# Two-layer decoder, the bridge into cross attention: cross keys are scaled and squared from their PSUM banks, with two more banks and a new written order

## What is computed

```python
x = x + self_attention(layernorm(x))                 # 32 heads of 16, causal, ALiBi
# cross attention: 32 query heads and 8 key/value heads of 128 features, no mask in effect
q = rmsnorm(layernorm(x) @ q_proj_w.T, q_norm_w)     # per head
k = rmsnorm(ctx @ k_proj_w.T, k_norm_w)              # per head, this is what is changed
v = ctx @ v_proj_w.T
x = x + softmax(q @ k.T / sqrt(128)) @ v @ o_proj_w.T
# rmsnorm(t, w) = w * t / sqrt(mean(t * t) + 1e-5)
```

## Time and profile before

| | |
|---|---|
| median of three runs | 1003.66 us (998.44 to 1005.22) |
| the profiled execution | 1004.14 us, its span 1002.4 us |
| mean granted TensorE clock | 0.970 |
| busy share of the span | PE 90%, DVE 83%, POOL 67%, ACT 63%, PE weight loads 47% |

### The profile page before, as it was taken

How to read it: one execution, slowest core, us unless ns; L and a number is a source line. 1 busy time by engine, 2 the same in 40 slices (tenths; PEclk the granted TensorE clock), 3 DMA queues, 4 the chain that set the end, 5 groups by cost and what they waited for, 6 DMA issues and landing times. The chain is left out here.

```text
span 1002.4 us, 21446 instructions
## 1 busy us (share of the span) xinstructions
PE 900.7 (90%) x6397; PEld 466.2 (47%) x6504; DVE 832.7 (83%) x2090; ACT 635.4 (63%) x1786; POOL 673.8 (67%) x689
## 2 busy tenths in 40 slices
PE   3979997799799999999999999999677887999977
PEld 1445544344344555455555545554234454655543
DVE  6998887689985889899999999898489887777685
ACT  4788887643453666676666767666243487887551
POOL 5897878677783666667666666666086687565583
PEclk9899999799999999999999999999979999999999
DMA  8799999867543666655555555666344499776665
GB/s 350 177 180 160 165 166 184 198 102 164 92 87 93 126 119 125 119 114 126 126 126 116 118 119 126 120 127 117 83 113 106 68 169 157 144 140 117 123 131 147
DMA packets 384304, 136.32 MB, mean 136 GB/s; under 512 B 369760, under 2 KB 370400, under 8 KB 381792
## 3 DMA queue, kind: packets, MB, share of 16 engines
q1 hardware_dynamic: 384224, 135.39, 65.7%
HBM read 42.01 MB, written 2.10 MB: 44 GB/s over the span
## 5 line engine op out<-in xcount | busy, mean ns | idle before, releaser
L157 PE MATMUL bank<-w_hi,hT 128*128 128x512 f16 (+2 forms) x1024 | 319.6, 370 | 16.7 <-DVE big L903 5.7
L157 PE MATMUL bank<-w_hi,small 128*128 128x512 f16 x512 | 164.0, 382 | 9.0 <-DVE small L1561 7.9
L157 PE MATMUL bank<-w_lo,hT 128*128 128x512 bf16 (+2 forms) x458 | 167.5, 368 | 0.0
L157 PEld LDWEIGHTS bank<-w_hi,hT 128*128 128x128 f16 (+1 forms) x1024 | 100.5, 99 | 117.2 <-issue 21.3
L1387 POOL TENSOR_TENSOR small<-small,mhalf 128x4 f32<-128x4 f32 x64 | 64.8, 1013 | 134.1 <-DVE small L980 134.1
L667 POOL TENSOR_TENSOR big<-big 128x512 f16<-128x512 f32 x96 | 112.8, 1182 | 33.8 <-DVE big L946 20.2
L1488 ACT ACTIVATE small<-small 128x128 f32<-128x128 f32 x256 | 98.8, 390 | 0.0
L157 PE MATMUL bank<-w_lo,small 128*128 128x512 bf16 x235 | 89.8, 382 | 0.0
L1403 POOL TENSOR_TENSOR w_lo<-stage,w_hi 128x512 bf16<-128x512 f32 x64 | 84.8, 1325 | 1.1 <-ACT w_hi L1524 1.1
L829 ACT ACTIVATE big<-bank,small 128x128 f32<-128x128 f32 x256 | 72.0, 377 | 20.7 <-DVE small L935 20.6
L1540 DVE TENSOR_TENSOR small<-small 128x512 f16<-128x512 f32 x64 | 79.4, 1240 | 4.6 <-ACT small L1483 4.4
(11 more groups left out here) (208 smaller groups left out, 2146.9 us busy)
## 6 DMA issues: line engine op xcount, KB each, us to landing
stage<-in_weights SPq DMA_DIRECT2D x16, 1024.0 KB, 5.7
stage<-in_weights SPq DMA_DIRECT2D x64, 256.0 KB, 2.9
big<-big SPq DMA_TRANSPOSE x168, 3.4
small<-in_ctxT SPq DMA_DIRECT2D x2, 1024.0 KB, 9.0
big<-in_ctx SPq DMA_DIRECT2D x2, 1024.0 KB, 5.7
out<-x SPq DMA_DIRECT2D x8, 256.0 KB, 2.4
big<-in_vectors SPq DMA_DIRECT2D x5, 256.0 KB, 9.7
x<-in_x SPq DMA_DIRECT2D x2, 512.0 KB, 5.5
```

The lines of the kernel that those rows point to most:

```text
L157: last = nc.tensor.matmul(out, lhs(a, c), rhs(b, c), start=start and n == 0, stop=stop and n == 3 * chunks - 1)
```

## The change

1. `key_scale` reads the key bank itself and not `kf[m]`. `key_stats` takes one factor from the bank and the other from `kf[m]`, so `key_take` stays. `rms_stats` gets a second source; the cross queries pass the same tile twice, as before.
2. `key_take` waits for the squares of batch b - 1 (`squares`) and no longer for `scaled`.
3. The product of `key(m, b)` waits for `scaled` of the last user of its bank and no longer for `k_taken`. Batches 0 to 3 use banks 4 and 5. From batch 4 on even batches use banks 6 and 7, odd ones 4 and 5, so the last user is then two batches back; `key_0_4` waits for the last `o_taken`. The first scores of the cross loop wait for all `scaled`.
4. Two guards are added, on `key_root` (the last `key_scale` of this m has read the root) and on `key_stats` (the last root has read the sums).
5. In the opening the product `k` of a batch waits for that batch's rows too, as `q` did.
6. All five lists of `BRIDGE_ORDER` are replaced. They hold the same steps.

```diff
-                if n == 0 and what == "q" and isinstance(b, int):
+                if n == 0 and what in ("q", "k") and isinstance(b, int):
                     opening.wait_rows(pe, b)
...
-def rms_stats(nc, dve, src, junk, ss, eps_out, chain, k):
+def rms_stats(nc, dve, src, again, junk, ss, eps_out, chain, k):
...
-        last = nc.vector.tensor_tensor_reduce(out=junk[:, at], in0=src[:, at], in1=src[:, at], scale=1.0, scalar=0.0,
+        last = nc.vector.tensor_tensor_reduce(out=junk[:, at], in0=src[:, at], in1=again[:, at], scale=1.0, scalar=0.0,
...
+FEW = 3
...
+    def key_bank(self, m, b):
+
+        return self.kbank[m if b <= FEW or b % 2 else 2 + m]
...
             if what == "key_root":
                 pool.wait_ge(self.var, b * 2 + (m + 1))
+                after(pool, self.scaled, b * 2 + (m - 1))
...
-                after(pe, self.k_taken, b * 2 + (m - 1))
-                product(self.nc, self.kbank[m][:], context(self.chip, b), columns(self.chip.weight(self.k_slots[m])),
+                if b == FEW + 1:
+                    pe.wait_ge(layer.signals["o_taken"], NB * 2)
+                else:
+                    last_user = b - 1 if b <= FEW else b - 2
+                    after(pe, self.scaled, last_user * 2 + (m + 1))
+                product(self.nc, self.key_bank(m, b)[:], context(self.chip, b), columns(self.chip.weight(self.k_slots[m])),
...
             if what == "key_take":
                 act.wait_ge(self.k_done, b * 2 + (m + 1))
-                after(act, self.scaled, b * 2 + (m - 1))
-                nc.scalar.activation(self.kf[m], self.kbank[m][:], ACT.Copy).then_inc(self.k_taken, 1)
+                after(act, self.squares, b * 2 + (m - 1))
+                nc.scalar.activation(self.kf[m], self.key_bank(m, b)[:], ACT.Copy).then_inc(self.k_taken, 1)
...
             if what == "key_stats":
                 dve.wait_ge(self.k_taken, b * 2 + (m + 1))
-                rms_stats(nc, dve, self.kf[m], self.junk, self.ss[m], self.ve[m], self.squares,
+                after(dve, self.root, b * 2 + (m - 1))
+                rms_stats(nc, dve, self.key_bank(m, b), self.kf[m], self.junk, self.ss[m], self.ve[m], self.squares,
                           b * 2 + m).then_inc(self.var, 1)
...
-                    last = nc.vector.scalar_tensor_tensor(out=self.kw[m][:, at], in0=self.kf[m][:, at],
+                    last = nc.vector.scalar_tensor_tensor(out=self.kw[m][:, at], in0=self.key_bank(m, b)[:, at],
...
-                     k_banks=chip.psum[4:6], v_banks=chip.psum[2:4], cols=chip.st[:, 0:34])
+                     k_banks=chip.psum[4:8], v_banks=chip.psum[2:4], cols=chip.st[:, 0:34])
...
-                    pe.wait_ge(keys.k_taken, 2 * NB)
+                    pe.wait_ge(keys.scaled, 2 * NB)
```

Of the lists, TensorE's from the last batch's first scores on, and the stretches of the other engines' that matter in the text below:

```diff
     "tensor": """
...
-        pv_0_6 out_0_5 scores_7_6 pv_1_6 out_1_5 out_2_5 out_3_5 scores_0_7 pv_2_6 scores_1_7 p_turn_7_6 scores_2_7
-        pv_3_6 pv_4_6 v_0_7 scores_3_7 pv_5_6 v_1_7 v_2_7 v_3_7 scores_4_7 scores_5_7 pv_6_6 pv_7_6 scores_6_7
-        scores_7_7 pv_0_7 pv_1_7 pv_2_7 p_turn_7_7 pv_3_7 key_0_0 key_1_0 key_0_1 key_1_1 value_0_0 out_0_6 key_0_2
-        out_1_6 out_2_6 out_3_6 pv_4_7 pv_5_7 key_1_2 pv_6_7 pv_7_7 key_0_3 key_1_3 key_0_4 value_1_0 out_0_7 out_1_7
-        out_2_7 out_3_7 slot_q_0_0 key_1_4 key_0_5 slot_q_0_1 key_1_5 value_1_1 key_0_6 key_1_6 value_0_1 key_0_7
-        key_1_7 value_1_2 value_0_2 slot_q_0_2 value_1_3 value_0_3 slot_scores_0_0 slot_q_0_3 slot_scores_0_1 value_0_4
-        slot_q_0_4 slot_scores_0_2 slot_q_0_5 value_1_4 value_0_5 value_1_5 value_0_6 value_1_6 value_0_7 value_1_7
...
+        scores_7_6 out_0_5 out_1_5 pv_0_6 out_2_5 scores_0_7 out_3_5 scores_1_7 pv_1_6 v_0_7 pv_2_6 scores_2_7
+        scores_3_7 p_turn_7_6 pv_3_6 v_1_7 v_2_7 v_3_7 scores_4_7 pv_4_6 pv_5_6 scores_5_7 pv_6_6 pv_7_6 scores_6_7
+        scores_7_7 pv_0_7 pv_1_7 p_turn_7_7 pv_2_7 pv_3_7 value_0_0 key_0_0 key_1_0 out_0_6 out_1_6 out_2_6 pv_4_7
+        key_0_1 pv_5_7 pv_6_7 out_3_6 pv_7_7 key_1_1 value_1_0 key_0_2 key_1_2 out_0_7 out_1_7 out_2_7 out_3_7 key_0_3
+        slot_q_0_0 key_1_3 key_0_4 key_1_4 key_0_5 slot_q_0_1 key_1_5 value_0_1 key_0_6 value_1_1 key_1_6 key_0_7
+        value_1_2 key_1_7 value_0_2 slot_q_0_2 value_1_3 value_0_3 value_1_4 value_0_4 slot_scores_0_0 slot_q_0_3
+        slot_scores_0_1 slot_q_0_4 value_0_5 slot_scores_0_2 slot_q_0_5 value_1_5 value_0_6 value_1_6 value_0_7
+        value_1_7
...
     "scalar": """
...
-        exp_6_6 norm_hi_0_0 p_hi_6_6 exp_7_6 weight_hi_0_7 value_weight_hi_0_0 exp_0_7 value_weight_hi_1_0 exp_1_7
...
+        norm_hi_0_0 exp_6_6 k_hi_1_7 exp_7_6 v_hi_1_6 exp_0_7 value_weight_hi_0_0 exp_1_7 p_hi_6_6 value_weight_hi_1_0
...
     "gpsimd": """
...
-        v_lo_0_7 o_lo_0_6 value_weight_lo_1_0 weight_lo_0_7 p_lo_4_7 norm_root_0_2 value_weight_lo_3_0 norm_lo_0_1
...
+        p_lo_3_7 weight_lo_0_7 v_lo_0_7 o_lo_0_6 value_weight_lo_3_0 v_lo_1_7 norm_lo_0_1 norm_root_0_2 o_lo_1_6
```

More of the change, by code:

```diff
@@ new lines @@
+        key_scale_1_0 key_stats_0_1 o_take_1_7 key_scale_0_1 key_stats_1_1 norm_z_0_3 x_add_0_6 key_scale_1_1
+        key_stats_0_2 norm_stats_0_4 key_scale_0_2 key_stats_1_2 x_add_0_7 key_scale_1_2 norm_z_0_4 slot_q_0_0
+        key_stats_0_3 key_stats_1_3 key_scale_0_3 key_stats_0_4 norm_stats_0_5 value_lo_0_0 key_scale_1_3 key_stats_1_4
+        key_stats_0_5 key_scale_0_4 norm_z_0_5 key_scale_1_4 value_lo_1_0 norm_stats_0_6 value_lo_0_1 key_stats_1_5
+        key_scale_0_5 slot_q_split_0_0 norm_z_0_6 key_stats_0_6 key_scale_1_5 value_lo_1_1 key_stats_1_6 key_stats_0_7
@@ new lines @@
+        key_scale_0_6 key_scale_1_6 slot_q_0_1 key_stats_1_7 value_lo_1_2 value_lo_0_2 key_scale_0_7 norm_stats_0_7
+        key_scale_1_7 slot_q_split_0_1 value_lo_1_3 value_lo_0_3 norm_z_0_7 slot_q_0_2 slot_scores_0_0 slot_q_split_0_2
+        value_lo_0_4 slot_q_0_3 slot_norm_0_0 slot_scores_0_1 slot_q_split_0_3 slot_p_split_0_0 slot_q_0_4 value_lo_1_4
+        value_lo_0_5 slot_norm_0_1 slot_scores_0_2 slot_q_split_0_4 slot_p_split_0_1 value_lo_1_5 value_lo_0_6
+        slot_q_0_5 value_lo_1_6 value_lo_0_7 value_lo_1_7
@@ new lines @@
+        value_weight_hi_1_1 key_take_0_0 query_weight_hi_0_0 o_hi_0_7 key_take_1_0 value_weight_hi_2_1 norm_hi_0_2
+        query_weight_hi_1_0 key_hi_0_0 query_weight_hi_2_0 key_take_0_1 value_weight_hi_3_1 query_weight_hi_3_0
+        key_hi_1_0 key_take_1_1 o_hi_1_7 norm_hi_0_3 key_hi_0_1 key_take_0_2 key_take_1_2 key_hi_1_1 slot_q_0_0
+        key_take_0_3 key_hi_0_2 key_take_1_3 key_hi_1_2 query_weight_hi_0_1 value_hi_1_0 key_take_0_4 norm_hi_0_4
+        key_hi_0_3 value_hi_0_0 key_take_1_4 key_take_0_5 key_hi_1_3 key_take_1_5 key_hi_0_4 value_hi_0_1
@@ new lines @@
+        key_lo_0_0 value_weight_lo_3_1 key_root_0_1 key_lo_1_0 query_weight_lo_0_0 o_lo_1_7 key_root_1_1
+        query_weight_lo_1_0 norm_lo_0_3 key_lo_0_1 key_root_0_2 query_weight_lo_2_0 query_weight_lo_3_0 key_lo_1_1
+        norm_root_0_4 key_root_1_2 key_lo_0_2 key_root_0_3 query_weight_lo_0_1 key_lo_1_2 norm_lo_0_4 key_root_1_3
+        key_root_0_4 key_lo_0_3 key_root_1_4 norm_root_0_5 key_lo_1_3 key_root_0_5 slot_q_0_0 key_lo_0_4 norm_root_0_6
+        key_lo_1_4 norm_lo_0_5 key_root_1_5 key_lo_0_5 key_root_0_6 key_lo_1_5 key_root_1_6 query_weight_lo_1_1
@@ new lines @@
+        p_turn_0_7 p_turn_1_7 p_turn_2_7 p_turn_3_7 value_load_0_1 query_load_0_0 norm_turn_0_1 o_turn_0_6 p_turn_4_7
+        p_turn_5_7 p_turn_6_7 norm_turn_0_2 key_turn_0_0 key_turn_1_0 o_turn_0_7 query_load_0_1 key_turn_0_1
+        norm_turn_0_3 key_turn_1_1 key_turn_0_2 next_load_0_0 key_turn_1_2 norm_turn_0_4 key_turn_0_3 key_turn_1_3
+        key_turn_0_4 key_turn_1_4 norm_turn_0_5 slot_q_split_0_0 key_turn_0_5 key_turn_1_5 key_turn_0_6 key_turn_1_6
+        norm_turn_0_6 key_turn_0_7 key_turn_1_7 slot_q_split_0_1 slot_q_split_0_2 norm_turn_0_7 slot_q_split_0_3
@@ L1057 @@
+        slot_p_split_0_0 slot_q_split_0_4 next_load_0_1 slot_p_split_0_1 slot_load_0_0
     """,
 }
+FEW = 3
 class CrossKeys:
@@ L1536, in step @@
                 dve.wait_ge(a.free, a.done)
-                rms_stats(nc, dve, qf, junk_, ss, ve, squares, k).then_inc(var, 1)
+                rms_stats(nc, dve, qf, qf, junk_, ss, ve, squares, k).then_inc(var, 1)
             if what == "q_split":
```

73 lines of the change are left out of this document (23 added, 50 removed).

## The result

| | before | changed |
|---|---|---|
| median, first comparison | 1003.97 us (998.44 to 1010.47, 10 runs) | 992.88 us (989.94 to 996.72, 10 runs) |
| ratio, 95% interval | | 0.9894 [0.9869, 0.9918] |
| median, second comparison | 1001.70 us (999.23 to 1007.56, 25 runs) | 994.00 us (990.24 to 997.51, 10 runs) |
| ratio, 95% interval | | 0.9917 [0.9888, 0.9945] |
| profiled execution, span | 1004.14, 1002.4 us | 996.72, 994.9 us; second 990.61, 988.8 us |

The change makes the kernel about 1% faster, 11.1 us in one comparison and 7.7 in the other. 996.5 was forecast, with 990.5 to 1002.5 as range. The second comparison repeats the changed kernel. Expected before it ran: a median of 991 to 995, a bridge (first cross product to loop) of 110.5 to 111.5 us without a gap at a reuse, and a start between 189 and 199 us. All of it came.

A forecast was written before the change was run, and what follows sets the result against it. TensorE was taken as the bound, with 10.6 us idle in the bridge to win at most. 1.2 at the start plus 7.6 of gaps less 1.5 of stalls gave 7.3 us, forecast 996.5 us, range 990.5 to 1002.5.

The forecast's parts named there:

- Near 22 us in all: Sign of being right: total time of the key_scale instructions on VectorE after the change, from 34.6 us before.
- 7.6 - 1.5 = 6.1 us less: Bridge after its start: 7.6 us of TensorE gaps go, 1.5 us of stalls at bank reuses are added.
- that nothing here touches: Bridge: 1.5 us of TensorE idle time expected to stay after the change.
- two like them of about 1 us: Bridge: two TensorE gaps like those at 254.09 and 275.45, together 2.0 us, expected to go with VectorE's saving.
- 1.5 us of stalls at the reuses: Bridge: allowance for TensorE waiting at all six bank reuses, key_0_1 to key_1_3, 1.5 us added.
- 1.2 us earlier: Start of the bridge: TensorE begins at 193.5 in place of 194.70, with value_0_0 ahead of key_0_0.
- the tail, counted as 0: Self-attention tail: last exponential at 191.8 as before, so no gain or loss; bounds -1.5 and +2 us.
- a first cross product later than 194.7: Sign of being wrong: TensorE's first product of the bridge starting after 194.7 us.
- a loop near 307: Sign of being right: the first matmul of the cross loop near 307 in place of 314.8 us.
- (b): Rival: TensorE also escapes the low clock after the tail's stall, another 3 to 5 us, about 992; chance 0.20.
- (c): Rival: VectorE's time is saved but TensorE's bridge gaps stay, 9.1 us, time 1002.5; chance 0.17.
- (d): Rival: key banks bind through late GpSimd roots at six reuses, at or over the old time; chance 0.08.

The follow-up runs named there:

- e1: The changed kernel with the five order lists of before; banks, operands and waits stay as changed: 1009.5 us.
- e3: The changed kernel with key_scale reading an SBUF copy again, three copy tiles in rotation, order and banks kept: 1003.98 us.
- e6: The changed kernel with both factors of the key squares from the SBUF copy, key_scale still reading the bank: 995.9 us.
- e11: The changed kernel with p_hi_6_6 moved ahead of exp_0_7 and the value weight's first split behind exp_1_7 on ScalarE: 993.74 us.
- e9: The changed kernel with 2.0 us of GpSimd work added ahead of each of the first six key roots: 1004.63 us.
- e7: The changed kernel with key_scale and both factors of the key squares reading SBUF copies, order and banks kept: 1005.84 us.
- e8: The changed kernel with one pair of key banks for all batches and two key_scale steps moved one step earlier: 1022.9 us.

## Why the prediction was right, and where it was not

- **The bound.** That TensorE's idle time is all there is to win held: busy 109 us before and in both profiles of the changed kernel, and 8.8 of the 9.2 us that the bridge lost are idle time. The rest did not move beyond its spread: 687.6 us behind the bridge before, 686.5 and 684.9 after. The experiments add what the prediction had no term for: a stop can cost more than its length, through the clock (some 3 us of e1's 15.7).
- **key_scale.** 347 ns and 16.3 us less were forecast; 342 and 16.7 came (34.6 - 17.9). "Near 22 us in all" was off, since four such instructions overlap to 1.13 us, as the prediction itself had it for one reuse: 17.9. e3 shows that the operand's place does it. The rule of the Trainium skill (SBUF — State Buffer, Who interferes with whom) that a VectorE instruction with at most one SBUF input, outside the two-port modes, escapes the contention is borne out for key_scale by 342 against 546 and 650 ns. L980, with one SBUF input, is held all the same (last section), and no run shows whether it is in such a mode. The 65 ns for a PSUM source, an estimate from the 120 and 58 cycles of the Trainium skill (VectorE: DVE Perf Modes, section on the TRN2 errata), do not show: 342 with the bank, 347 the median without.
- **Squares.** 280 forecast, 287 measured. VectorE fell from 100.7 to 81.0 us in the bridge, 80 was forecast. In time they were worth 2 us (e6). In part that was given back by L980, 277 ns before and 448 after (2.7 us), by the same kind of hold-up (last section).
- **The sum.** From first cross product to loop it said 7.6 - 1.5 = 6.1 us less; 9.2 and 9.4 came. Two terms were mis-sized. The 1.5 us "that nothing here touches" went too: half of it was small waits of the same kind, 0.35 us at 224.21 for key_take and 0.40 at 285.13 for value_lo, the rest waits of 0.22 us and less. Of the "two like them of about 1 us" one, 0.95 us at 268.17, waited for value_lo; the other, 0.78 at 291.94, for ScalarE's copy of a query product (L1478); both went. The 1.5 us of stalls at the reuses were zero: margins laid out by hand at 0.4, 1.2, 2.5, 0.8, 0.8 and 2.6 us came out at 0.53, 0.66, 1.90, 0.28, 0.96 and 1.30, smaller than thought at four places, but a positive margin costs nothing, and the allowance for it was a hedge inside the sum.
- **The start.** 1.2 us earlier was forecast. By the first row as common mark the first product came 28.8 us after it, against 27.9 before: 0.9 later. Two steps lie in this. That value_0_0 need not wait for the last probability tile was right: from the end of the last exponential to the first product it took 3.00 us before, 1.92 and 1.80 after, 1.1 to 1.2 less. The step that failed is the tail, counted as 0 with "the last exp comes out at 191.8 by hand as before": it ended 24.9 us after the mark before and 26.8 and 26.9 after, 2.0 later, beyond the bound of 1.5. The last split of the value weight, which was to be done by about 191, ran from 195.47 on GpSimd (L1141), but it held nobody up: it ended at 196.63 and TensorE, with its own work until then, began at 197.51 without a gap. Timeline of ScalarE, the last exponentials before and then after:

```profile
189.52 2.18 ACT L829 ACTIVATE big<-bank,small 128x128 f32<-128x128 f32 x8 [0.19 <-DVE small L935]
...
194.44 1.14 ACT L829 ACTIVATE big<-bank,small 128x128 f32<-128x128 f32 x4 [0.41 <-DVE small L935]
```

  That ScalarE's new order is the cause is likely: with the old order of e1 the last exponential ends 24.5 us after the mark, and with e11's two moves on ScalarE 24.4. Which of the two moves does it is open.
- **Together** +3.2 in the bridge and -2.1 at the start leave the forecast 1.1 us high on this reckoning (7.3 against 8.4). That it came so near is in part luck, since two errors of 2 and 3 us cancel in part. The comparisons give 11.1 and 7.7, mean 9.4; the difference lies within the spread of one execution.
- **Signs.** Named as a sign of being wrong was a first cross product later than 194.7, and as one of being right a loop near 307. The profiles have 197.51 and 193.19, 308.45 and 303.95: the whole kernel up to there wanders by more than the sign, so it decides nothing; by the common mark it would have been a true sign.
- **Rivals.** (b) was named for a time near 992, and the time came without it: matmuls of 0.59 to 0.63 us still stand from 197.51 to 201, and the stretch from 193 to 233 us has a clock of 0.90, against 0.94 before. A number near a rival's is not that rival. (c) is excluded, no gap stayed. (d) was near: GpSimd's root later by 2.0 us gives +10 us of bridge (e9) and the time of before, where the arithmetic of (d), six times 2.0 less 1.2 of margin, would have said 4.8 (it had the queue behind the root and the clock out of account); and e1 shows that the same banks with another order are slower than before. I gave it 0.08 from margins; with four margins under 1 us it deserved more.

## What to carry to other kernels

Operands moved from SBUF to a PSUM bank save the hold-up by GpSimd (602 to 342 ns here) but keep the bank busy through the whole chain, so the order must put that chain's length of other products between two uses. An order written out by hand, its waits and its buffers are one thing: each alone was worth nothing (e3, e7) or less (e1, e8) against the kernel before, and one misfit propagates through every in-order queue. A stop of TensorE can cost more than its length, since matmuls behind it may run at the lower clock. Cut each profile at marks that all kernels have, before reading a difference of some microseconds out of two spans.
